# Two gated layers on one core: each scatter of the routed rows waits for the landing of the one before it

## The reference, cut to what matters

```
logits = xf @ router_w.T + router_b            # 2048 tokens, 16 experts
top_w, top_e = top_k(softmax(logits), 2)
top_w = top_w / sum(top_w)
for each expert e:
    h  = silu(xf @ W1[e].T) * (xf @ W3[e].T)
    y  = h @ W2[e].T
    yn = layernorm(y) * g[e] + b[e]
    out += (top_w where top_e == e) * yn
```

## Time and profile before

| | |
|---|---|
| timed runs, median (lowest to highest) | 886.46 us (882.73 to 886.53) |
| profiled execution, span from first to last instruction | 918.4 us |
| the profiled execution's own time | none shown beside the span |
| 32 scatters to xg_scratch | start 711.1 to 751.0 us |
| first load from xg_scratch | starts 795.1 us |
| TensorE busy / VectorE / ScalarE / GpSimd | 77% / 70% / 54% / 43% of the span |

### The profile page before, as it was taken

One profiled execution on the slowest core, in us unless ns is written; L12 is line 12 of the kernel. 1 busy time (PEld: TensorE's weight loads), 2 busy tenths in 40 slices (PEclk: granted clock), 3 DMA queues, 4 the chain that ended last, 5 costly groups with the idle time before them and its releaser, 6 DMA issues.

```text
span 918.4 us, 20712 instructions
## 1 busy us (share of the span) xinstructions
PE 708.3 (77%) x7336; PEld 530.8 (58%) x7351; DVE 642.1 (70%) x1521; ACT 496.9 (54%) x893; POOL 392.0 (43%) x470
## 2 busy tenths in 40 slices
PE   4688887689899867998997798999859309798830
PEld 1456554457676734676675466658646207698830
DVE  5586776697869775977986797787658325476645
ACT  2444555465666753656676566655726205487711
POOL 7351633560714063434412760480041750068880
PEclk9789999899999997999999999999978759799975
DMA  8600000000000000000000000000023313122104
GB/s 206 177 1 1 1 1 1 1 1 3 1 2 1 2 1 3 2 1 2 1 2 1 1 1 2 1 2 2 1 87 87 119 42 128 36 70 70 62 35 146
DMA packets 43839, 30.03 MB, mean 33 GB/s; under 512 B 7650, under 2 KB 41692, under 8 KB 43484
## 3 DMA queue, kind: packets, MB, share of 16 engines
q1 hardware_dynamic: 39932, 23.17, 8.7%
q0 software_dynamic: 2560, 5.25, 1.5%
q10 hardware_dynamic: 1248, 0.28, 0.2%
HBM read 18.98 MB, written 9.44 MB: 31 GB/s over the span
## 4 chain that ended last, share of the span: by engine, by line
PE 38%; DVE 24%; issue 13%; POOL 13%; ACT 6%; another core or an unknown queue 4%; DMA 1%; DVEq 1%; POOLq 0%; ACTq 0%; SPq 0%
PE psM L841 14%; DVE arena L1538 5%; PE psO L926 4%; ACT arena L1208 4%; DVE PR L1426 4%; PE psT L884 4%; POOL yt_scratch L1918 3%; PE psS L875 3%; PE psS L911 3%; POOL arena L1895 3%; POOL arena L1892 3%; POOL RS L1871 2%; DVE MX L1420 2%; DVE arena L1546 2%
## 5 line engine op out<-in xcount | busy, mean ns | idle before, releaser
L841 PE MATMUL psM<-arena 128*128 128x128 f32 (+7 forms) x1168 | 267.9, 372 | 44.1 <-DVE arena L1538 25.3
L1208 ACT ACTIVATE arena<-psT 128x512 f32<-128x512 f32 (+2 forms) x296 | 150.8, 530 | 153.9 <-PE psT L1003 37.1
L841 PEld LDWEIGHTS psM<-arena 128*128 128x128 f32 (+5 forms) x1168 | 155.5, 190 | 93.0 <-DVE arena L1538 38.1
L1208 ACT ACTIVATE arena<-psM 128x512 f32<-128x512 f32 (+2 forms) x168 | 88.3, 543 | 114.3 <-PE psM L841 113.3
L1420 DVE TENSOR_REDUCE MX<-psS 128x4 f32<-128x512 f32 (+1 forms) x160 | 102.7, 682 | 62.5 <-issue 24.0
L1870 POOL TENSOR_SCALAR RS<-MV 128x2 f32<-128x2 f32 x56 | 14.4, 256 | 293.2 <-DVE MV L1574 167.5
L1892 POOL TENSOR_TENSOR arena<-arena,powm 128x8 f32<-128x8 f32 x64 | 109.9, 1717 | 5.3
L1208 ACT ACTIVATE PR<-PR 128x512 f32<-128x512 f32 x160 | 94.6, 626 | 21.1 <-DVE PR L1426 20.9
L1426 DVE TENSOR_TENSOR PR<-psS,MX 128x512 f32<-128x512 f32 x160 | 102.1, 678 | 0.0
L884 PE MATMUL psT<-ident,PR 128*128 128x128 f32 x640 | 94.3, 282 | 5.4 <-ACT PR L1208 1.9
L884 PEld LDWEIGHTS psT<-ident,PR 128*128 128x128 f32 x640 | 74.9, 145 | 34.1 <-issue 27.0
(11 more groups left out here) (198 smaller groups left out, 1163.8 us busy)
## 6 DMA issues: line engine op xcount, KB each, us to landing
arena<-in_L_ffn_w SPq DMA_DIRECT2D x50, 128.0 KB
xg_scratch<-zeros SPq DMA_DIRECT2D x12, 256.0 KB, 3.7
arena<-xg_scratch SPq DMA_DIRECT2D x12, 256.0 KB
arena<-yt_scratch SPq DMA_DIRECT2D x4, 512.0 KB, 5.3
arena<-in_L_ffn_wqkv SPq DMA_DIRECT2D x2, 768.0 KB, 5.0
arena<-in_L_ffn_ln_g SPq DMA_DIRECT2D x1, 1024.0 KB, 5.3
arena<-in_L_ffn_ln_b SPq DMA_DIRECT2D x1, 1024.0 KB, 8.5
out<-arena SPq DMA_DIRECT2D x4, 256.0 KB, 2.2
```

Of the source, the lines that this page charges most:

```text
L841: return nc.tensor.matmul(o, lhsT, rhs, start=start, stop=stop)
L1208: return nc.scalar.activation(o, i, f, **kw)
```

## The change

Ahead of each scatter but the first, GpSimd now waits until the semaphore scattered shows that all scatters before it have landed. The transfers, their order and their contents are the same.

```diff
             pool.wait_ge(pos_done, 1)
             for t in range(NT):
                 for k in range(2):
+                    if t or k:
+
+                        pool.wait_ge(scattered, 16 * (2 * t + k))
                     G.indirect_dma_start(XG, bass.IndirectOffsetOnAxis(POSU[:, k, t:t + 1], 0), XN1ALL[:, t, :], None)\
                         .then_inc(scattered, 16)
             pool.drain().then_inc(b_over, 1)
```

## The result

The changed kernel takes a median of 930.53 us in four runs (929.43 to 934.22), beside 886.5 us for the kernel before in the same session (four runs, 882.73 to 888.35). The ratio is 1.0526, with an interval of 1.0478 to 1.0573. The two medians differ by 44.0 us, by themselves a ratio of 1.0497.

A forecast was written before the change was run, and what follows sets the result against it. Chained scatters were to set the routed-row loads' start: 711.06 + 31 x 3.0 = 804.1 us, plus 0.96 + 2.7 + 0.08 = 807.8, plus 123.3 = 931.1 us. The range was 896 to 945 us.

The forecast's parts named there:

- The reading of the stall: ScalarE's 32.0 us wait at 723 to 755 us: absent from timed runs, so their routed-row loads start at 763.2 us.
- rival 1: Before the routed-row loads: the stall is in timed runs too, so the change costs 12.7 us, 899.2 us; chance 0.20.
- rival 3: At the scatters: their dense sequence causes the stall, spacing removes it, steps are short; 884.3 us, not slower; chance 0.06.
- The price of a step: From one scatter's start to the next one's: two terms, 3.11 us together, rounded down to 3.0 us.
- first term: Within a scatter step, from start to landing as a waiter sees it: 2.22 us, from the later loop's last scatter.
- second term: Within a scatter step, from landing to the next start: 0.89 us, as for the first scatter, released by a semaphore.
- Contention: Scatters beside weight loads: costed at nothing; ten landings at 3.7 us would add 15 us, put into the range only.
- The second way to 931 us: Timed runs: routed-row load moves from 763.2 to 807.8 us, 44.6 us on top of 886.5.
- The terms behind the scatters: After the last scatter's start: 0.96 us busy, 2.7 to drain's end, 0.08 to the load, 123.3 to the end.
- The cover: Before the change, scatters lie wholly beside other work: GpSimd's drain ends at 754.6 us, loads start at 763.2 without stall.
- Rival 2: At the scatters: next one prepared ahead of its wait, only 0.30 us paid, 2.52 us a step; 916.2 us; chance 0.11.
- Rival 4: At the scatters: long steps of 3.6 us or more, beside weight loads or from cold starts; 949.7 us; chance 0.08.

The follow-up runs named there:

- experiment 1: The kernel before, unchanged, profiled once more: 886.98 us, ratio 1.0011.
- experiment 6: The kernel before with only the loads of ln_g and ln_b moved behind those of expert 3, as a control: 886.35 us, ratio 1.0011.
- Experiments 5 to 7: Changed kernel with the ln_g and ln_b loads issued earlier, 926.22 us; kernel before with the same edit, 886.35 us; changed kernel again, 933.49 us.
- experiments 3 and 4: Kernel before with the wait at its last 12 scatters only, 904.87 us, and at the 12 behind the first only, 908.94 us.

## Why the prediction came out at 931 us

**The reading of the stall was right, its length was not.** The stall belonged to one execution. The second profile of the kernel before doesn't have it, and no timed run of that kernel is long enough to hold it (the longest took 891.64 us). Taking it off decided between 899 and 931 us. But with the load of before at 763.2 us, the prediction had it 52.1 us after the first scatter (711.06 us), and it comes after 47.2 us in experiment 1 and after 46.0 us in experiment 6. The prediction took off one wait of 31.99 us. The same chain has two more pieces with that releaser, 2.49 us ahead of it and one behind it:

```profile
755.21 1.38 another core or an unknown queue
```

With all three, 35.9 us, the load would stand at 759.2 us, 48.2 us after the first scatter. The changed kernel agrees: VectorE was to be done at about 763 us, and its drain ends at 757.9 us, 45.9 us after the first scatter.

```profile
L1753 DVEq DRAIN  x1: 537/537/537, 757.4 to 757.4; - x1
```

That 32.0 us of stall and 31.9 us of gap were so nearly equal says less than was made of it, since the gap set a span against timed runs, and each later execution took 2.2 us longer than its span. What held up that one execution stays open: it came once and was not seen again, so no run could take it apart. With the stall fall rival 1, which added 12.7 us to the timed runs, and rival 3, which needed a stall that the dense scatters cause.

**The price of a step: its first term was right, its second was not.** From a start to the landing were 2.22 us, as taken from the later loop. From the landing to the next start were 0.27 us and not 0.89 us. The failed step is "the new wait makes every scatter such a one": the first scatter's 0.89 us is not the price of a wait. In the changed kernel it is there once, as 0.84 us ahead of the first scatter, and 31 times it is not. Why the first pays it was not tried. By the prediction's own test, "a step under 2.6 us makes the second term wrong", it was wrong: 2.49 us a step, 31 x 0.51 = 15.8 us too much in the sum.

**Contention was costed at nothing, and is 11.0 us.** The prediction had up to 15 us for it in its range and none in its sum. Of the 11.0 us, 3.2 us go with scatters that were themselves busy longer. Experiments 5 to 7 show about half of it, 5.3 us, to come from two loads of SyncE. The rest, 5.7 us, has its place (beside weight loads and VectorE's pieces) but was not taken apart.

So the mean step was 88.2 / 31 = 2.85 us where 3.0 was taken: two terms were mis-sized in opposite directions, -15.8 and +11.0 us. The first scatter started 1.0 us later than in the profile of before. The load came at 804.0 us instead of 807.8, and the end at 927.2 us of span. The own time of the execution is 2.2 us longer than its span, which the prediction took for the time itself. The second way to 931 us, 44.6 us on top of 886.5, had an error on each side too: from the first scatter to the load it put 96.7 us in the changed kernel (92.0 measured) and 52.1 us in the one before (47.2 measured). Each is too long by almost 5 us, and the difference, 44.8 us measured, hides it. So the mechanism was right, a chain of landings that sets the start of the loads, but that 931 stands so close to 930.53 is in part luck.

**The terms behind the scatters were right.** The drain ended 3.66 us after the last scatter's start (0.96 + 2.7 = 3.66 taken), then 0.08 us to the load; from the load to the end it was 123.2 us (123.3 taken). Nothing had to be added for the clock: 0.89 in the first 25 us of the last phase, against 0.86 before.

**The cover was thinner than shown.** The prediction's figures put GpSimd's end 763.2 - 754.6 = 8.6 us before the load of an execution without a stall. It is 2.6 us in experiment 1 and 1.2 us in experiment 6. Most of the difference is again the place of the load. GpSimd's drain ended 43.5 us after the first scatter in the profile with the stall and 44.4 us after it in experiment 1, while the load comes after 47.2 us and not after 52.1. It didn't enter the sum, but a smaller added wait would have been misjudged by it.

**The other rivals.** Rival 2 had the right step, 2.52 against 2.49 us, and the wrong time, 916.2 us, since it too left contention out. The rule of the Trainium skill that stood beside it ("DMA: Bandwidth & Descriptors", "Anatomy of one DMA — SWDGE (gpsimd) path") gives an estimate of 2.15 us for such a transfer. This case's quiet landings agree at 2.22 us, those under load (3.73 and 6.51 us) do not, and the step has 0.27 us more. Rival 4, at 3.6 us a step or more, was met by single steps only (4.00 and 6.77 us).

## What to carry to other kernels

Chaining transfers turns work that took its issue time (here 1.26 us) into work that takes its landing time (2.49 us), and exposes each landing to whatever else the DMA engines carry at that moment; with four in flight the same waits cost nothing that could be measured here. Before a long unexplained wait in a profile goes into a sum, the span is to be held against the timed runs: what none of them has room for is not the kernel's price. When such a stretch is taken off, every piece of it goes, not only the longest. And how much slack a piece has is read from executions without a stall, more than one, since here it was 2.6 us in one and 1.2 us in another.

## What the runs showed of the hardware that was not expected

- A scatter of 64 KB lands after 2.22 us with little else under way (DMA share 0.08) and after 6.51 us at a share of 0.76. The waiter then starts the next one 0.27 us later, in both cases. The DMA share is not all that counts: one landed after 4.39 us at a share of 0.04 (experiments 3 and 4).
- A scatter's own busy time on GpSimd grows from 0.96 to as much as 1.86 us in the changed kernel beside some pieces of VectorE, though not beside each of them. The scatters of 724.09 and 752.06 us stand beside these rows of VectorE's timeline:

```profile
724.05 0.95 DVE L1733 TENSOR_TENSOR arena<-arena 128x768 bf16<-128x768 f32 x1
...
748.47 4.62 DVE L1743 TENSOR_TENSOR arena<-arena 128x1024 bf16<-128x1024 f32 x4
```

```profile
724.09 1.74 POOL L1949 DMA_INDIRECT xg_scratch<-XN1ALL,POSU  x1 [1.65 <-DMA xg_scratch<-XN1ALL,POSU]
...
752.06 1.86 POOL L1949 DMA_INDIRECT xg_scratch<-XN1ALL,POSU  x1 [1.54 <-DMA xg_scratch<-XN1ALL,POSU]
```

  In the second profile of the kernel before, a scatter beside the same piece, L1733, took no longer than any other:

```profile
727.03 0.95 DVE L1733 TENSOR_TENSOR arena<-arena 128x768 bf16<-128x768 f32 x1
```

```profile
726.99 0.96 POOL L1946 DMA_INDIRECT xg_scratch<-XN1ALL,POSU  x1 [0.30 <-issue]
```

  The Trainium skill ("Advanced Engine Details and Errata", "GPSIMD Details") says that GpSimd shares a read and a write interface with VectorE and conflicts with instructions of two inputs in SBUF, or in a mode that takes both ports. The two longer scatters fit this, the third does not by itself, and no run took the VectorE pieces away, so the cause is not shown.
- GpSimd's drain ends 3.6 to 3.7 us after the start of the last scatter, whether the scatters before it were chained or dense (800.28 to 803.94 us here, 755.8 to 759.5 us in the second profile of before).
